# Layer normalisation of the last stage of a graph network: rows scaled on GpSimd instead of ScalarE

## The reference

```python
def _layernorm(x, axis=-1, eps=1e-05):
    m = jnp.mean(x, axis=axis, keepdims=True)
    v = jnp.var(x, axis=axis, keepdims=True)
    return (x - m) / jnp.sqrt(v + eps)

x = _layernorm(x + two graph-attention layers(x))      # 4 heads, softmax over each node's edges, relu
...
# second block: a message per edge, the maximum per destination, and a two-layer network on each node
msgs = z[edge_dst] @ Wd + z[edge_src] @ Ws + edge_weight[:, None] * ww[None, :] + bm
agg = jax.ops.segment_max(msgs, edge_dst, num_segments=n)
hidden = jax.nn.relu(z @ W1a + agg @ W1b + b1)
x = _layernorm(x + hidden @ W2 + b2)
```

## Time and profile before

| what | value |
|---|---|
| median of three timed runs | 6749.88 us |
| span of the profiled execution | 6748.4 us |
| the median above that span | 1.5 us |
| PE / DVE / ACT / POOL busy over the whole span | 75% / 61% / 69% / 72% |
| last stage, steady part (6645 to 6693 us): PE / DVE / ACT / POOL | 37.6 / 38.2 / 47.2 / 12.8 us of 48 |

### The profile page before, as it was taken

How to read it: one execution, slowest core, us unless ns; L and a number is a source line. 1 busy time by engine, 2 the same in 40 slices (tenths; PEclk the granted TensorE clock), 3 DMA queues, 4 the chain that set the end, 5 groups by cost and what they waited for, 6 DMA issues and landing times.

```text
span 6748.4 us, 155294 instructions
## 1 busy us (share of the span) xinstructions
PE 5090.5 (75%) x24591; PEld 4768.5 (71%) x24591; DVE 4120.4 (61%) x11944; ACT 4661.7 (69%) x10625; POOL 4883.6 (72%) x5157
## 2 busy tenths in 40 slices
PE   7988888888887798888888888755555556556567
PEld 6988888888886788888888888744454545455455
DVE  4655555555556465555555555665666666666677
ACT  4877777777776687777777777674555555555558
POOL 6777777777775777777777777557777777777772
PEclk6555555555556655555555555567888888888889
DMA  7333333333332433333333333265666666666664
GB/s 207 91 94 88 88 91 93 89 91 93 88 92 54 128 93 88 89 90 93 89 90 93 88 88 95 63 188 159 167 173 169 174 172 171 175 171 175 167 184 137
DMA packets 731832, 814.08 MB, mean 121 GB/s; under 512 B 176926, under 2 KB 545694, under 8 KB 730670
## 3 DMA queue, kind: packets, MB, share of 16 engines
q1 hardware_dynamic: 570110, 471.14, 24.9%
q0 software_dynamic: 158240, 331.14, 20.8%
q10 hardware_dynamic: 2448, 0.74, 0.0%
HBM read 753.64 MB, written 48.89 MB: 119 GB/s over the span
## 4 chain that ended last, share of the span: by engine, by line
POOL 18%; PE 18%; issue 11%; DVE 8%; DMA 7%; SPq 2%; DVEq 1%; ACT 1%; POOLq 0%; ACTq 0%
POOL G L836 18%; PE bS L982 6%; PE bA L947 6%; DVE acc L1631 3%; DMA st<-d_neg 3%; DMA G<-ztable,idx 2%; DMA G<-table,idx 2%; DVE bA L1873 1%; PE bM L982 1%; PE bE L982 1%; DVE ch L1879 1%; PE bA L857 1%; PE bE L857 1%; SPq L451 1%; DVEq L1631 1%
## 5 line engine op out<-in xcount | busy, mean ns | idle before, releaser
L836 POOL DMA_INDIRECT G<-table,idx x3286 | 3104.7, 945 | 1022.5 <-issue 905.1
L982 PE MATMUL bS<-G,S 128*128 x8816 | 2036.9, 391 | 378.8 <-DVE acc L1631 202.8
L1248 ACT ACTIVATE S<-iota_row,nd 128x128 f32<-128x128 f32 x5904 | 1868.1, 387 | 501.4 <-issue 310.4
L982 PEld LDWEIGHTS bS<-G,S 128*128 128x128 f32 x8816 | 1749.8, 280 | 501.7 <-issue 493.9
L836 POOL DMA_INDIRECT G<-ztable,idx x1643 | 1550.4, 944 | 518.8 <-issue 462.3
L947 PEld LDWEIGHTS bA<-adst,st 128*128 128x128 f32 x7872 | 1797.1, 333 | 120.3 <-issue 116.4
L947 PE MATMUL bA<-adst,st 128*128 x7872 | 1698.9, 340 | 83.8 <-issue 70.3
L1631 DVE TENSOR_TENSOR acc<-acc,bS 128x136 f32 (+1 forms) x4408 | 1279.1, 290 | 567.0 <-DVE acc L1631 82.6
L1252 ACT ACTIVATE S<-S,one_col 128x512 f32<-128x512 f32 x1476 | 1065.2, 722 | 47.9
L1227 ACT ACTIVATE st<-xd,neg_p 128x512 f32<-128x512 bf16 x972 | 690.1, 710 | 490.5 <-PE bA L947 330.8
L857 PE MATMUL bA<-ident,G 128*128 128x128 f32 x1646 | 321.1, 335 | 645.8 <-DVE ch L1879 546.1
(11 more groups left out here) (223 smaller groups left out, 3668.0 us busy)
## 6 DMA issues: line engine op xcount, KB each, us to landing
xd<-d_drel SPq DMA_DIRECT2D x328, 384.0 KB
xd<-in_ew SPq DMA_DIRECT2D x312, 256.0 KB
st<-d_neg SPq DMA_DIRECT2D x312, 256.0 KB
wide<-table SPq DMA_DIRECT2D x4608, 0.5 KB
G<-table,idx POOLq DMA_INDIRECT x3286
isend<-in_ew SPq DMA_DIRECT2D x104, 256.0 KB
isend<-d_neg SPq DMA_DIRECT2D x104, 256.0 KB
G<-ztable,idx POOLq DMA_INDIRECT x1643
```

The source lines that it names most:

```text
L836: pool.indirect_dma_start(G[:, r, c, 0:width], None, from_table, bass.IndirectOffsetOnAxis(ap=idx[:, r, c:c + 1], axis=0)).then_inc(gather ...
L982: mm = pe.matmul(bank_of(l, u, r, k)[:, j * w:(j + 1) * w], S[:, onehots(r, i), s, :], Gf[:, bass.ds(chunk_at[0][s], w)], start=True, stop ...
L1248: step = act.activation(S[:, onehots(r, i), s, :], iota_row[:, :], ACT.Abs, bias=nd[:, r, i * QS + s:i * QS + s + 1])
```

## The change

In the last stage ScalarE's `normalize` is gone. GpSimd does the same with two instructions a group: the rows of the whole group times `rstd`, then plus `nmr`, each of these read once a tile and repeated over the 128 features. The second waits for the first by a semaphore, and counts up `f_y` as ScalarE did. GpSimd's loop does the normalisation of group g - 4 ahead of the bias of group g. ScalarE's loop loses one turn at its end.

```diff
+            def normal_rows(g):
+                n = tiles_of(g)
+                rows = OF[:, g % 4, 0:n]
+                pool.wait_ge(f_norm, g + 1)
+                pool.tensor_tensor(rows, rows, rstd[:, g % 2, 0:n].unsqueeze(2).to_broadcast([P, n, HID]), ALU.mult).then_inc(weighted, 1)
+                pool.wait_ge(weighted, NG + g + 1)
+                pool.tensor_tensor(rows, rows, nmr[:, g % 2, 0:n].unsqueeze(2).to_broadcast([P, n, HID]), ALU.add).then_inc(f_y, 1)
...
-            for g in range(NG):
-                final_rows(g)
+            for g in range(NG + 4):
+                if g >= 4:
+                    normal_rows(g - 4)
+                if g < NG:
+                    final_rows(g)
...
-                def normalize(g):
-                    act.wait_ge(f_norm, g + 1)
-                    for j in range(tiles_of(g)):
-                        rows = OF[:, g % 4, j, :]
-                        step = act.activation(rows, rows, ACT.Identity, bias=nmr[:, g % 2, j:j + 1], scale=rstd[:, g % 2, j:j + 1])
-                    step.then_inc(f_y, 1)
...
-                for g in range(NG + 5):
+                for g in range(NG + 4):
...
-                    if g >= 5:
-                        normalize(g - 5)
```

## The result

The changed kernel takes 6763.92 us (median of 12 runs, 6761.06 to 6766.41), the kernel before in the same comparison 6749.68 (12 runs). The ratio is 1.0022, with a 95% interval of 1.0015 to 1.003: 14 us slower, where 2 were forecast and the range ended at 6758.5.

The account below looks back on a forecast made before the run. VectorE was taken to bound the last stage at 4.80 us a group. Nothing per turn and +2.0 us at the end gave 6750.4 us profiled; with the median 1.5 above, 6751.9 us, range 6747.5 to 6758.5.

Parts of the forecast that it names:

- What bounds the stage: Last stage: VectorE sets the pace at 4.80 us a group; removing ScalarE's 1.54 us gives 0 per turn.
- the 0.41 us gap: Before each VectorE turn: fetching the quad's four tile offsets into registers, not waiting for TensorE's product in `bS`.
- The price of the new instructions: GpSimd's two added instructions a group: 1.05 us each, bounds 1.05 and 1.57; steady work 3.46 of 4.80 us.
- The port: GpSimd and VectorE's L1938 excluding each other at SBUF: 0 in steady turns, blocked L1938 from group 20 on.
- the waits for `f_y`: SyncE's store, released some 2.3 us after `f_norm`, goes out earlier; L1937 waits for it two groups later; no cost counted.
- rival 2: Steady turns: a slow `zrow` load makes L811 block VectorE's L1938; at 6 us, +10, 6762 us; chance 0.08.
- The two stores behind are the same: End of the stage: the stores behind the last normalisation stay unchanged, adding nothing to the +2.0 us.
- The backlog: Last groups: GpSimd falls behind VectorE and ends at 6748.05 against ScalarE's 6746.01, +2.0 us.
- Rival 3: Steady turns: GpSimd becomes the bound above 1.72 us an instruction; at 2.0, +21, 6771 us; chance 0.03.
- the pair without a bias: End of the stage: GpSimd's two normalising instructions once no biases are left, 2.14 us a group.
- the price of 1.57: Upper bound for each new GpSimd instruction, 1.57 us: the end comes 5.2 us later, +7.2 in all.

Follow-up runs that it names:

- e4: Changed kernel, but each store waits for the next group's f_norm and ScalarE normalises groups 19 to 24; 6748.6 us against 6748.9 before, ratio 1.0.
- p1: Kernel before, but VectorE fetches the next quad's tile offsets while its statistics run; 6742.1 us against 6748.9 before, ratio 0.9989.
- p2: e4, but VectorE fetches the next quad's tile offsets while its statistics run; 6740.5 us against 6748.9 before, ratio 0.9987.
- e2: Kernel before, but SyncE stores each group one turn later, directly behind the load of zrow; 6765.7 us against 6757.8 before, ratio 1.0012.
- e3: Changed kernel, but ScalarE normalises groups 19 to 24 as before, GpSimd only 0 to 18; 6763.2 us against 6757.8 before, ratio 1.0008.
- e6: Changed kernel, but the load of zh also waits for f_norm, leaving only the store ahead; 6763.9 us against 6748.9 before, ratio 1.0022.
- e1: Changed kernel, but SyncE's store of each group also waits for the next group's f_norm; 6766.6 us against 6757.8 before, ratio 1.0013.
- e7: Kernel before, but the next group's zh load goes directly behind zrow's, the store staying late; 10289 us against 10288 before, ratio 1.0005.

## Why the prediction was wrong, point by point

**What bounds the stage: right.** VectorE kept the pace, and 1.54 us less on ScalarE gave nothing (e4). I read the 0.41 us gap rightly as the fetch of offsets; p1 and p2 show it.

**The price of the new instructions: right.** 1.04 us for the forecast 1.05; 3.4 us a turn of 4.80. The port: right too; L1940 was 0.16 in the steady part, and 0.73, 0.99 and 0.85 at the end, where I had placed it.

**The step that failed first** is that of the waits for `f_y`: "it now comes some 2.3 us after `f_norm` [...] so the store goes out earlier". That was seen and priced at nothing; the only danger I looked for in it was a late load of `zrow` (rival 2), which did not come. The load of `zrow` landed in at most 3.1 us, where rival 2 needed 4.9. The runs put a late register load in its place, about 0.4 us in 15 of 19 turns, 5.6 to 6.5 us. The trace of before could have shown it. Over its whole span the same load takes up to 1.0 us:

```profile
L1488 DVEq TENSOR_LOAD <-regs_sel x1476: 337/343/995, 158.2 to 6728.3; - x185
```

Nineteen of these 1476 loads take over 0.45 us. Fourteen of them lie in the node parts of the two attention layers, and each has a store out of SBUF issued 1.3 to 2.4 us ahead of it; a few loads there with such a store ahead are not late. In one of the fourteen GpSimd has just ended its last instruction, so that nothing of it runs beside the load:

```profile
L1488 DVEq TENSOR_LOAD <-regs_sel x1: 893/893/893, 4404.2 to 4404.2; - x1
```
```profile
4402.84 0.41 SPq L655 DMA_DIRECT2D zrow<-acc  x1
```

The first row is that load (start 4404.2), the second SyncE's timeline with the store, 1.4 us ahead.

**The second step that failed** is "The two stores behind are the same", the end. The backlog was right, 2.3 us for the forecast 2.0. But what follows GpSimd's last normalising instruction was taken to be only the stores, as it was behind ScalarE's. GpSimd's own closing instruction is a drain of 9.6 us (9.7 in the trace of before, at 6737.1, hidden), and 6.8 us of it now lie bare. Moving the last work to another engine also moves that engine's ending onto the path.

**The range** took its upper end from the bounds of the GpSimd price alone, so it missed both. Rival 3, GpSimd as the bound, had the right engine and the wrong reason. Two slips in the sum change nothing: the pair without a bias is put at 2.14 us where its own rows give 2.18 (measured: 2.15), and the price of 1.57 by itself gives 6757.1 us, not the 6758.5 at which the range ends.

## What to carry to other kernels

When a step gets faster or changes engines, list what its semaphore releases, and for each transfer that now starts earlier ask which short instruction of the pacing engine's queue it will meet; register loads are such instructions, and no view of busy time shows them. Before moving the last work of a program to an engine, look at how that engine's program ends. And if the engine that was relieved is not the one that sets the pace, relieve that one as well, in the same edit.

## What the runs showed of the hardware

A register load of four values from SBUF on VectorE takes 0.34 us. Where a 256 KB store out of SBUF was issued 1.0 us ahead, 64 of 71 took 0.50 to 0.85 us (changed kernel, e2, e3, e6). In p1 it was late at 0.86, 1.10 and 1.35 us and not at 0.61 or less nor at 1.59 or more; that is one turn at each distance, and `zh` loads moved along with the stores, so these edges are rough. In the node part of layer 1 a load was still 0.52 us long with its nearest store 1.7 us ahead. A store issued 0.2 us behind the load's start (before, e1) or a load of the same size into SBUF at the same place (e7) does no harm, and neither does SyncE's issuing of a transfer at that moment as such: in p2 the loads start 0.03 us behind the issue of `zrow` and take 0.34. Why the direction decides is not shown. Of the four loads spared in the changed kernel the first has no store ahead of it, and at the other three the store's issue took 0.60 to 0.76 us in place of 0.53; but e2 and e6 each spared one behind an issue of 0.53, which stays unexplained.

GpSimd's closing drain takes 8.9 to 9.7 us in all profiled executions, whether it starts 128 us (p2) or 154 us (changed kernel) behind the issue of the last gather, so its length hardly depends on that. What it does in this time was not tried.
